# Projections of a gated linear attention layer: biases held in the centred weights' last row, and the norms of q and k as a power on GpSimd

## What is computed

```python
q = silu(hs @ Wq + bq)      # (tokens, 16 * 64); k, v alike
g = hs @ Wg + bg            # used later as silu(g)
beta = sigmoid(hs @ Wb + bb)
q = q * rsqrt(sum(q * q, per head) + 1e-06)
k = k * rsqrt(sum(k * k, per head) + 1e-06)
```

## Time and profile before

| | |
|---|---|
| median of 3 runs | 3186.0 us (3183.77 to 3191.86) |
| the profiled execution, its own time | 3187.53 us |
| its span in the profile | 3185.7 us |
| mean granted TensorE clock | 0.956 of full speed |
| busy share of the span: PE, DVE, ACT, POOL | 87%, 75%, 50%, 43% |
| the projection loop | about 206 to 498 us of the span |
| DMA, mean over the span | 91 GB/s |

### The profile page before, as it was taken

How to read it: one execution, slowest core, us unless ns; L and a number is a source line. 1 busy time by engine, 2 the same in 40 slices (tenths; PEclk the granted TensorE clock), 3 DMA queues, 4 the chain that set the end, 5 groups by cost and what they waited for, 6 DMA issues and landing times. The chain is left out here.

```text
span 3185.7 us, 74542 instructions
## 1 busy us (share of the span) xinstructions
PE 2756.1 (87%) x27685; PEld 1909.2 (60%) x27685; DVE 2394.1 (75%) x4439; ACT 1599.3 (50%) x3758; POOL 1359.5 (43%) x2167
## 2 busy tenths in 40 slices
PE   0889996759999999999999999999576588888888
PEld 0654444647777777777777777777474552222223
DVE  7868888938878688786877858866597467877775
ACT  0469996844343434343433434444285445555555
POOL 1112222125656556565555655655474214211111
PEclk9989997969999999999999999999799779999999
DMA  2026657851332313324233242232286312111111
GB/s 61 1 94 245 243 237 244 280 111 36 79 64 51 87 38 83 69 41 89 54 65 71 40 89 63 55 69 72 101 294 202 91 38 43 32 21 21 26 25 29
DMA packets 487649, 290.81 MB, mean 91 GB/s; under 512 B 402900, under 2 KB 447508, under 8 KB 478484
## 3 DMA queue, kind: packets, MB, share of 16 engines
q1 hardware_dynamic: 478070, 256.64, 29.9%
q10 hardware_dynamic: 4608, 16.78, 1.7%
q0 software_dynamic: 4608, 12.59, 1.2%
HBM read 155.92 MB, written 129.99 MB: 90 GB/s over the span
## 5 line engine op out<-in xcount | busy, mean ns | idle before, releaser
L2477 DVE TENSOR_REDUCE mx<-banks 128x2 f32<-128x1024 f32 (+3 forms) x384 | 358.1, 956 | 105.4 <-PE banks L1921 84.3
L2182 ACT ACTIVATE probs<-banks 128x1024 f32<-128x1024 f32 (+3 forms) x384 | 307.0, 810 | 245.0 <-PE banks L1943 237.9
L1148 ACT COPY xs<-banks 64x64 f32<-64x64 f32 (+2 forms) x640 | 166.1, 260 | 397.8 <-PE banks L980 394.8
L849 POOL TENSOR_SCALAR xc<-xc,halves 128x64 f32<-128x64 f32 (+1 forms) x256 | 191.8, 749 | 361.9 <-DVE xc L1328 349.3
L1707 POOL TENSOR_SCALAR_AFFINE_SELECT probs<-probs 128x256 f32<-128x256 f32 x256 | 103.7, 407 | 524.2 <-ACT probs L2182 524.0
L980 PE MATMUL banks<-xc,ssm 64*64 64x16 f32 (+2 forms) x5120 | 250.2, 217 | 36.9 <-issue 34.8
L980 PEld LDWEIGHTS banks<-xc,ssm 64*64 64x64 f32 x5120 | 209.8, 135 | 116.3 <-issue 57.5
L1800 PE MATMUL banks<-wproj,xnT 128*128 128x512 f32 x512 | 264.9, 599 | 0.6 <-DVEq L493 0.6
L1328 DVE SCALAR_TENSOR_TENSOR xc<-xc,halves,banks 64x64 f32<-64x64 f32 (+1 forms) x512 | 159.9, 312 | 112.5 <-PE banks L991 106.3
L1138 ACT COPY ssm<-banks 16x64 f32<-16x64 f32 (+2 forms) x896 | 215.9, 241 | 51.8 <-PE banks L952 39.7
L1173 ACT COPY ah<-banks 128x768 f32<-128x768 f32 x128 | 102.2, 798 | 257.6 <-PE banks L1012 257.6
(11 more groups left out here) (355 smaller groups left out, 6499.3 us busy)
## 6 DMA issues: line engine op xcount, KB each, us to landing
proj_s<-prj SPq DMA_DIRECT2D x32, 2048.0 KB, 6.8
qkv_t<-proj_s SPq DMA_DIRECT2D x32, 1536.0 KB
ka<-proj_s ACTq DMA_DIRECT2D x32, 512.0 KB, 5.0
mem_s<-o_sb SPq DMA_DIRECT2D x32, 512.0 KB, 2.6
om<-mem_s SPq DMA_DIRECT2D x32, 512.0 KB, 4.0
om<-proj_s SPq DMA_DIRECT2D x32, 512.0 KB, 4.8
nblk_s<-ssa POOLq DMA_DIRECT2D x32, 256.0 KB, 4.6
blk_s<-res SPq DMA_DIRECT2D x16, 512.0 KB, 4.2
```

The source lines that it names most:

```text
L849: pool.tensor_scalar(inverse_of(k, lv + 1)[:, :, w:2 * w], inverse_of(k, lv), halves[:, lv, 1:2], None, ALU.mult).then_inc(half_set, 1)
L1148: last = act.copy(xs[right, k % 2, 0:4 * (SUB << lv)], products(k, lv, out_)[right, :])
L2182: act.activation(probs[:, s % 2, :, at:at + w], slot_of((kind, s, k))[:, :, 0:w], ACT.Exp, scale=D1 ** -0.5).then_inc(b_read, 1)
L2477: dve.tensor_reduce(mx[:, s % 2, c, :, t:t + 1].rearrange("p e a -> p (e a)"), slot_of((kind, s, k))[:, :, 0:w], AX, ALU.max).then_inc(a_r ...
```

## The change

Three edits, all in the projections.

1. **Bias.** A row vector taken away from every row of a weight matrix changes nothing in the product with a token that sums to zero. So the last row of each projection matrix is subtracted from all its rows, on GpSimd, in one operation of 128 x 4096 (and one of 128 x 80 for the gates' weights). The last row is then zero; SP loads the biases there. The last row of `xnT` is set to 1 on GpSimd and left out of ScalarE's copies. The bf16 split, `ones3`, `bias3` and the eight bias matmuls per tile go. Five more loads, each one row broadcast to all partitions, bring the last rows (`wlast`, `wglast`).
2. **Norms.** No square root on ScalarE and no reciprocal on VectorE: GpSimd adds 1e-6, takes the power -0.5 with `tensor_tensor(..., ALU.pow)` on 128 x 32, and multiplies k's half by `sb_tok`. The factors of a tile are now made and used within the same round of the loop.
3. **v.** GpSimd scales v by `sb_tok` in place (1024 columns); VectorE scales q and k alone (2048 columns). The store also waits for v.

```diff
@@ SP, start
-            sp.dma_start(bias_p[:, :], a["bproj"].rearrange("a (p n) -> (a p) n", p=P)).then_inc(ld2, 16)
+            sp.dma_start(wglast[:, :], a["wgate"][D - 1:D, :].rearrange("a n -> (a n)").partition_broadcast(P)).then_inc(ld2, 16)
             for n, w in enumerate(("Wq", "Wk", "Wv", "Wg")):
                 sp.dma_start(wproj[:, HD * n:HD * n + HD], a[w]).then_inc(ld2, 16)
-            sp.wait_ge(bias_split, 5)
-            sp.dma_start(bias_s.rearrange("c (p n) -> p c n", p=P), bias_h[:, :, :]).then_inc(bias_out, 16)
-            sp.wait_ge(bias_out, 16)
-            sp.wait_ge(bias_set, 2)
-            sp.dma_start(bias3[0:3, :], bias_s).then_inc(bias_in, 16)
+            for n, w in enumerate(("Wq", "Wk", "Wv", "Wg")):
+                sp.dma_start(wlast[:, HD * n:HD * n + HD], a[w][D - 1:D, :].rearrange("a n -> (a n)").partition_broadcast(P)).then_inc(ld2, 16)
+            sp.wait_ge(w_centred, 2)
+            sp.dma_start(wproj[D - 1:D, :], a["bproj"]).then_inc(bias_in, 16)
@@ SP, loop
                 sp.wait_ge(p_normed, i + 1)
+                sp.wait_ge(v_scaled, i + 1)
@@ POOL, start
-            pool.memset(ones3[:, :], 1.0).then_inc(bias_set, 1)
-            pool.wait_ge(xq_done, 1)
-            pool.memset(bias3[:, :], 0.0).then_inc(bias_set, 1)
-            pool.wait_ge(ld2, 144)
-            split = Count(pool, bias_split)
...
+            pool.wait_ge(ld2, LD2)
+            pool.tensor_tensor(wgate[:, :], wgate[:, :], wglast[:, :], ALU.subtract).then_inc(w_centred, 1)
+            pool.tensor_tensor(wproj[:, :], wproj[:, :], wlast[:, :], ALU.subtract).then_inc(w_centred, 1)
+            pool.wait_ge(w_centred, 2)
+            pool.wait_ge(norm_done, 1)
+            pool.memset(xnT[3 * P // 4:P, :], 1.0).then_inc(xone_set, 1)
+            pool.wait_ge(xone_set, 1)
@@ POOL, loop
-            for i in range(T + 1):
-                if i >= 1:
-                    pool.wait_ge(v_prj, i + 1)
-                    pool.tensor_tensor(prj_f[:, i - 1, H0:2 * H0], prj_f[:, i - 1, H0:2 * H0], sb_tok[:, i - 1, :], ALU.mult).then_inc(p_sq, 1)
-                if i < T:
-                    pool.wait_ge(p_silu, 8 * i + 6)
-                    if i:
-                        pool.wait_ge(p_red, 3 * i)
-                    x = prj[:, i % 4, 2 * HD:3 * HD]
-                    pool.tensor_tensor(prj_sq[:, 2, :], x, x, ALU.mult).then_inc(p_sq, 1)
+            fac = Count(pool, p_std)
+            fac.link(pool.memset(prj_half[:, :], -0.5))
+            pool.wait_ge(sb_root, 1)
+            for i in range(T):
+                n, v = i % 2, prj[:, i % 4, 2 * HD:3 * HD]
+                pool.wait_ge(p_red, 2 * i + 2)
+                if i >= 2:
+                    pool.wait_ge(p_normed, i - 1)
+                fac.link(pool.tensor_scalar(prj_n[:, n, 1, :], prj_n[:, n, 0, :], 1e-6, None, ALU.add))
+                fac.link(pool.tensor_tensor(prj_f[:, n, :], prj_n[:, n, 1, :], prj_half[:, :], ALU.pow))
+                pool.tensor_tensor(prj_f[:, n, H0:2 * H0], prj_f[:, n, H0:2 * H0], sb_tok[:, i, :], ALU.mult).then_inc(v_prj, 1)
+                pool.wait_ge(p_silu, 8 * i + 6)
+                if i:
+                    pool.wait_ge(v_red, i)
+                pool.tensor_tensor(prj_sq[:, 2, :], v, v, ALU.mult).then_inc(p_sq, 1)
+                pool.wait_ge(p_sq, i + 1)
+                heads_v = v.rearrange("p (h d) -> p h d", d=DK)
+                pool.tensor_tensor(heads_v, heads_v, sb_tok[:, i, :].unsqueeze(2).to_broadcast([P, H0, DK]), ALU.mult).then_inc(v_scaled, 1)
@@ PE, loop
-                    pe.matmul(bank[n], xnT[:, P * i:P * i + P], wproj[:, 512 * n:512 * n + 512], start=True, stop=False)
-                    pe.matmul(bank[n], ones3[:, :], bias3[:, 512 * n:512 * n + 512], start=False, stop=True).then_inc(p_mm, 1)
+                    pe.matmul(bank[n], xnT[:, P * i:P * i + P], wproj[:, 512 * n:512 * n + 512], start=True, stop=True).then_inc(p_mm, 1)
@@ ACT, feed-forward phase
-                act.copy(xnT[:, 2 * P * p:2 * P * p + 2 * P], bank[0][:, 0:2 * P]).then_inc(xT_done, 1)
+                if p == 0:
+                    act.wait_ge(xone_set, 1)
+                act.copy(xnT[0:D - 1, 2 * P * p:2 * P * p + 2 * P], bank[0][0:D - 1, 0:2 * P]).then_inc(xT_done, 1)
@@ ACT, loop
-                            if i:
-                                act.wait_ge(p_red, 3 * i - 1)
-                                act.activation(prj_n[:, (i - 1) % 2, 1, :], prj_n[:, (i - 1) % 2, 0, :], ACT.Sqrt, bias=prj_eps[:, 0:1]).then_inc(p_std, 1)
...
+                    if n in (2, 4):
+                        w = n // 2 - 1
+                        act.wait_ge(p_silu, 8 * i + n)
+                        if i:
+                            act.wait_ge(p_red, 2 * i - 1 + w)
+                        act.activation(prj_sq[:, w, :], prj[:, i % 4, HD * w:HD * w + HD], ACT.Square).then_inc(p_sq_q, 1)
@@ DVE, loop
-                if i >= 1:
-                    dve.wait_ge(p_std, i)
-                    prc.link(dve.reciprocal(prj_f[:, i - 1, 0:2 * H0], prj_n[:, (i - 1) % 2, 1, :]))
...
+                if i < T:
+                    for w in range(2):
+                        dve.wait_ge(p_sq_q, 2 * i + w + 1)
+                        dve.tensor_reduce(prj_n[:, i % 2, 0, H0 * w:H0 * w + H0], prj_sq[:, w, :].rearrange("p (h d) -> p h d", d=DK), AX, ALU.add).then_inc(p_red, 1)
+                if i >= 1:
+                    dve.wait_ge(p_sq, i)
+                    dve.tensor_reduce(vv[:, i - 1, :], prj_sq[:, 2, :].rearrange("p (h d) -> p h d", d=DK), AX, ALU.add).then_inc(v_red, 1)
+                if i < T:
+                    dve.wait_ge(v_prj, i + 1)
+                    qk = prj[:, i % 4, 0:2 * HD].rearrange("p (h d) -> p h d", d=DK)
+                    dve.tensor_tensor(qk, qk, prj_f[:, i % 2, :].unsqueeze(2).to_broadcast([P, 2 * H0, DK]), ALU.mult).then_inc(p_normed, 1)
```

More of the change, by code:

```diff
@@ L43 @@
 ROUNDER = 1.5 * 2 ** 22
+LD2 = 16 * 13
 TIES_DOWN = 1.0 - 2.0 ** -22
@@ L97, in layer_kernel @@
         ys_s = dram("ys_s", (NT * P, D))
-        bias_s = nc.dram_tensor("bias_s", (3, 4 * HD), BF16, kind="Internal").ap()
         qk_s = nc.dram_tensor("qk_s", (2, 3, P, B * L), BF16, kind="Internal").ap()
@@ L130, in layer_kernel @@
         fa = sb("fa", [P, T * D], scope=s1)
-        above_fa = sb("above_fa", [P, T * D], scope=s1)
+        wlast = sb("wlast", [P, 4 * HD], scope=s1)
         fsc = sb("fsc", [P, 2, T * D // BLOCK], scope=s1)
@@ L146, in layer_kernel @@
         gates = sb("gates", [5 * H0, B * L], scope=sW)
-        ones3 = sb("ones3", [P, P], BF16, scope=sW)
         wgate = sb("wgate", [P, 5 * H0], scope=sW)
@@ L151, in layer_kernel @@
         sb_tok = sb("sb_tok", [P, T, H0], scope=sW)
-        bias_p = sb("bias_p", [P, 4 * HD // P], scope=sW)
-        bias_r = sb("bias_r", [P, 2, 4 * HD // P], scope=sW)
-        bias_h = sb("bias_h", [P, 3, 4 * HD // P], BF16, scope=sW)
+        wglast = sb("wglast", [P, 5 * H0], scope=sW)
         sW.close()
@@ L159, in layer_kernel @@
         s2 = ExitStack()
-        bias3 = sb("bias3", [P, 4 * HD], BF16, scope=s2)
+        below_sq = sb("below_sq", [P, 2 * HD], scope=s2)
         prj_sq = sb("prj_sq", [P, 3, HD], scope=s2)
@@ L163, in layer_kernel @@
         prj_n = sb("prj_n", [P, 2, 2, 2 * H0], scope=s2)
-        prj_f = sb("prj_f", [P, T, 3 * H0], scope=s2)
-        prj_eps = sb("prj_eps", [P, 1], scope=s2)
+        prj_f = sb("prj_f", [P, 2, 2 * H0], scope=s2)
+        prj_half = sb("prj_half", [P, 2 * H0], scope=s2)
         vv = sb("vv", [P, T, H0], scope=s2)
@@ L366, in layer_kernel @@
         p_red = sem("p_red")
+        v_red = sem("v_red")
+        v_scaled = sem("v_scaled")
         p_stored = [sem(f"p_stored{n}") for n in range(2)] + [hq_done, h_turned]
@@ L473, in layer_kernel @@
         bias_sems = [updated, mixed, squared, ratio_set]
-        bias_split, bias_out, bias_in, b_summed = bias_sems
+        w_centred, xone_set, bias_in, b_summed = bias_sems
         ffn_sems = [staged, x_turned, xT_done, gu_done, silu_done, hid_done]
@@ L1749, in gate_logits @@
                 if p == 0:
-                    pe.wait_ge(ld2, 144)
+                    pe.wait_ge(w_centred, 1)
                 else:
@@ L2059, in _ @@
             act.wait_ge(cleared, len(prj_sems))
[L2060 to L2067, removed]
-                            if i:
-                                act.wait_ge(p_red, 3 * i - 1)
-                                act.activation(prj_n[:, (i - 1) % 2, 1, :], prj_n[:, (i - 1) % 2, 0, :], ACT.Sqrt, bias=prj_eps[:, 0:1]).then_inc(p_std, 1)
-                            act.wait_ge(p_silu, 8 * i + 2)
-                            act.activation(prj_sq[:, 0, :], prj[:, i % 4, 0:HD], ACT.Square).then_inc(p_sq_q, 1)
-                        if n == 4:
-                            act.wait_ge(p_silu, 8 * i + 4)
-                            act.activation(prj_sq[:, 1, :], prj[:, i % 4, HD:2 * HD], ACT.Square).then_inc(p_sq_q, 1)
```

(41 more changed lines are left out.)

13 lines of the change are left out of this document (2 added, 11 removed).

## The result

The changed kernel is slower: **3307.9 us** median of 4 runs (3305.0 to 3321.6) against 3188.9 (3183.8 to 3192.8, 4 runs now) for the kernel before, ratio 1.038 with a 95% interval of [1.036, 1.040]. I had forecast 3172, in a range of 3135 to 3210. The profiled execution after took 3321.6 us, the longest of its four runs, with a span of 3319.8.

What follows compares the result with a forecast made beforehand. ScalarE, with two table loads in an 8.85 us round, was the bound, TensorE just behind. Rounds of 8.36 us and a start net +3.5 gave -13.9 us: 3187.5 to 3173.6, less 1.5 for the median, 3172 us; range 3135 to 3210.

Steps and rivals of the forecast that it cites:

- The power ... I take 1.1: Projection loop: GpSimd's power on 128 x 32, in no row, was taken to cost 1.1 us a round.
- Twice as many steps give 2.2, the far end: GpSimd's power in the loop: upper end of its assumed cost, 2.2 us, from doubling the steps assumed for 1.2.
- each 0.1 us of the power moves this by 3.2 us: Whole time: 32 powers, so each 0.1 us in one power's cost shifts the 3172 us forecast by 3.2 us.
- rival 1: Projection loop: VectorE's scaling starts before GpSimd's squares of v; 7.87 us a round, 3157 us in all; chance 0.27.
- the forecast's ring: Projection loop: GpSimd and VectorE wait for each other, squares, scaling, two sums, factors adding to 8.4 us a round against 8.85.
- GpSimd alone: 5.8 us: Projection loop: GpSimd's own operations in a round, power included, sum to 5.8 us, under TensorE's 6.9.
- rival 3: Projection loop: a dear power between k's sums and everything else makes the kernel slower, 3207 us at 2.2; chance 0.22.
- wrong altogether: Signs that would refute the forecast: a power of over 2.2 us, or products that do not hold each other.
- break-even of 1.53 us: Projection loop: cost of one GpSimd power at which the change's whole gain of 13.9 us is gone.
- +5.5: Start: GpSimd's 4096-column subtraction, after loads landing at about 25.0, holds VectorE's small operation, adding 5.5 us to the path.
- -2.0: Start: GpSimd's clearing of `bias3` goes, so a small VectorE operation is no longer held, saving 2.0 us.
- By that rule the terms below add up: GpSimd and VectorE: a two-input SBUF operation locks the shared port for its whole length; without this, 3130 us in all.

Runs made afterwards that it cites:

- the tables alone: Kernel before with ScalarE's square root and VectorE's reciprocal taken for two tiles in one instruction each, bias matmuls kept: 3183.9 us, ratio 0.998.
- the probes: Changed kernel plus one unused 128 x 1024 product of two SBUF inputs on VectorE in each round but the last, beside GpSimd's power: 3308.3 us.
- the second order: Bias edit with late subtraction, v on VectorE, factors used one tile later, GpSimd's addition and power directly behind the product releasing VectorE's scaling: 3260.9 us.

## Why the prediction was wrong

**The step that failed** is "The power ... I take 1.1", and with it "Twice as many steps give 2.2, the far end". It measured 5.46, five times the forecast and two and a half times its far end. I had carried over the ratio of a reciprocal to a plain operation from VectorE to GpSimd, and called the result a bound; it was an analogy, and no row showed it. (Its own working ends at 1.2, not 1.1, which would move the sum by 3 us.) The runs show 158 ns a column where three assumed functions made about 31. The forecast's own price list shows that nothing else of size was wrong: "each 0.1 us of the power moves this by 3.2 us" gives 3172 + 43.6 x 3.2 = 3311.5; measured were 3307.9, and a product in its place gave 3143.8 where the list gives 3172 - 8.5 x 3.2 = 3145. Agreement to 1 us in the second is partly luck: half of those rounds ran in rival 1's order, and the mean round was 7.26 us where the forecast's ring makes 7.5.

**Point by point.**
- ScalarE bounds the kernel before, with TensorE just behind: right. With the bias edit alone the round stays at 8.85, with the tables alone it falls to TensorE's 8.59.
- The ring and who is first in it: right. Squares 1.89 ahead, scaling 3.97, v 3.83; 12.48 us against 8.36 - 1.1 + 5.46 = 12.7.
- "GpSimd alone: 5.8 us" and the far end of the sum were sound as arithmetic, and worthless with the wrong power.
- The rivals: the ending that came is rival 3, in its place and by its mechanism, and of the signs listed in advance one of "wrong altogether" came, a power of over 2.2 us. The rival's break-even of 1.53 us fits too: a line through the run with the product (0.25) and the changed kernel (5.46) crosses the time before at about 1.7. Its price was cut off at 2.2, so the range ended at 3210. The text itself said that "nothing here bounds it from above for sure". A range that held would have had to say what that sentence means in microseconds. I would now give this case more than 0.22, since the operation had no row.
- The start: +5.5 was 7.35. The loads landed at 27.0, not 25.0 (the last broadcast row landed 11.1 us after its issue at 15.9), and the hold is longer by as much. -2.0 was right.
- The end: no cost, right; the clearing of `gl` ends at 629.8 and the next phase begins at 630.8.
- "By that rule the terms below add up": right for additions and products, wrong for the power. The Trainium skill, page "SBUF — State Buffer", section "SBUF: two separate sides", has the shared ports locked for the whole instruction. Rows agree for a plain product of 1024 columns (3.83 and 3.97 here), and the probes disagree for the power of 32 columns: 1.21 us within its 5.46. The measurement decides. In the changed kernel this made no difference, since VectorE had nothing to run there.

## What to carry to other kernels

Where a change rests on an operation that no row shows, its price is the forecast: measure it by itself first, or let the range say that it may be several times as dear (here five). An instruction in a ring of two engines costs its whole length; the same instruction beside the other engine's work counts only in its own engine's list. Look at the order before giving up the operation, and at which engine's instruction starts first where two of them meet and one must stand still. Taking work from the second-slowest engine pays only once the slowest is relieved.

## What the runs showed that I had not expected

- GpSimd's power takes 2.93 us for 16 columns and 5.46 for 32, some 158 ns a column. The 5.46 is the same in all seven kernels that have it, alone and beside VectorE's sums, the probe and the scaling.
- It holds VectorE's two-input operations off neither in the middle (1.21 us for the probe) nor shortly after its start (3.39 for the scaling that starts 0.08 behind it, against 3.35 before the change). GpSimd's one-input addition of 32 columns, on the other hand, stands still until VectorE's scaling ends: 3.29 instead of 0.29 us, and 3.46 in the second order. I did not try whether a power that starts after VectorE's scaling waits for it as well.
- The same instructions in two orders made 96 us of the whole time (3260.9 and 3164.5): what differs is whether the addition or the power meets VectorE's scaling. The addition came 0.05 us behind the scaling; what would happen if it came first, no run shows.
